# Chunked cross-attention on one core: SP issues a period's transfers in another order, two of them paced by the query projections

## What is computed

```python
def proj(t, W, b):
    t = t.transpose(0, 2, 1) @ W.T + b
    return t.reshape(N, nc, CHUNK, H, Dh)
qh = proj(q, Wq, bq); kh = proj(k, Wk, bk); vh = proj(v, Wv, bv)      # q = k = v = ctx
scores = jnp.einsum('bnqhd,bnkhd->bnhqk', qh, kh) * scale
scores = scores + jnp.where(km[:, :, None, None, :] > 0, 0.0, NEG)    # km: the mask by chunk
attn = jax.nn.softmax(scores, axis=-1)
out = jnp.einsum('bnhqk,bnkhd->bnqhd', attn, vh).reshape(N, T, C)
out = (out @ W_out.T + b_out).transpose(0, 2, 1) * masks
out = out + x
mu = jnp.mean(out, axis=2, keepdims=True)
var = jnp.mean(jnp.square(out - mu), axis=2, keepdims=True)
return (out - mu) * jax.lax.rsqrt(var + EPS)
```

## Time and profile before

| | us |
|---|---|
| median of 3 runs | 2022.49 |
| lowest and highest of them | 2009.72, 2039.61 |
| the profiled execution | 2028.28 |
| its span, first to last instruction | 2026.4 |

### The profile page before, as it was taken

The page is one execution under the profiler, slowest core; times in us unless marked ns, Lnnn a source line. Parts: engine busy times, 40 slices in busy tenths (PEclk is TensorE's granted clock), DMA queues, the critical chain, the costliest instruction groups (busy, mean ns, idle before and its releaser), DMA issues.

```text
span 2026.4 us, 90376 instructions
## 1 busy us (share of the span) xinstructions
PE 1919.8 (95%) x40488; PEld 1624.1 (80%) x40488; DVE 1703.8 (84%) x1577; ACT 1331.6 (66%) x1792; POOL 1503.6 (74%) x1059
## 2 busy tenths in 40 slices
PE   7999999999999999999999999999999999989994
PEld 6887888878788887888788888787877888878783
DVE  4887988888888887889888888887888889878796
ACT  5766766667666666766666676676666767766672
POOL 4777778777777877777777777777777778767774
PEclk9999999999999999999999999999999999999997
DMA  5667878778777887777878778787877878868666
GB/s 167 170 169 195 216 209 217 200 203 215 207 193 212 216 222 186 197 203 210 212 198 216 208 211 211 198 221 202 208 189 195 213 200 214 225 189 213 193 170 194
DMA packets 242880, 409.59 MB, mean 202 GB/s; under 512 B 28992, under 2 KB 94784, under 8 KB 242496
## 3 DMA queue, kind: packets, MB, share of 16 engines
q1 hardware_dynamic: 242496, 403.82, 75.6%
HBM read 168.82 MB, written 67.11 MB: 116 GB/s over the span
## 4 chain that ended last, share of the span: by engine, by line
PE 91%; issue 4%; DVE 2%; DMA 1%; SPq 1%; ACT 0%; POOL 0%; DVEq 0%
PE proj_bank L308 36%; PE proj_bank L365 18%; PE proj_bank L342 18%; PE score_bank L381 10%; PE o_bank L414 9%; DMA prob_t<-squares 1%; SPq L256 1%; DVE squares L668 0%; DMA b_cols<-b_in 0%; ACT prob L473 0%; DVE stats L695 0%; ACT score_bank L465 0%; DVE sums L652 0%; DVE y L686 0%; POOL prob L552 0%
## 5 line engine op out<-in xcount | busy, mean ns | idle before, releaser
L552 POOL TENSOR_TENSOR prob<-prob,recip 128x1024 f32<-128x1024 f32 x256 | 481.9, 1903 | 46.9 <-DVE recip L660 46.9
L570 POOL TENSOR_TENSOR y<-y,x_raw 128x512 f32<-128x512 f32 x256 | 330.7, 1292 | 238.4 <-DVE y L686 238.4
L560 POOL TENSOR_TENSOR ctx_lo<-ctx_raw,ctx_hi 128x512 fp32r<-128x512 f32 x255 | 330.3, 1295 | 200.3 <-ACT ctx_hi L453 187.9
L495 ACT ACTIVATE k_f<-proj_bank,b_cols 128x512 f32<-128x512 f32 x256 | 176.5, 689 | 388.3 <-PE proj_bank L308 388.3
L641 DVE TENSOR_REDUCE row_max<-score_bank 128x32 f32<-128x2048 f32 x128 | 293.3, 2292 | 162.9 <-PE score_bank L381 162.9
L308 PE MATMUL proj_bank<-ctx_hi,w_hi 128*128 128x512 f32 x1024 | 338.7, 412 | 2.9 <-DVE ctx_lo L625 2.9
L308 PE MATMUL proj_bank<-ctx_hi,w_lo 128*128 128x512 f32 x1024 | 323.3, 397 | 2.2 <-issue 2.2
L308 PE MATMUL proj_bank<-ctx_lo,w_hi 128*128 128x512 f32 x1024 | 322.2, 395 | 0.0
L652 DVE TENSOR_REDUCE sums<-prob 128x16 f32<-128x1024 f32 x256 | 309.3, 1209 | 4.2 <-ACT prob L473 4.2
L668 DVE STREAM_TRANSPOSE squares<-prob 128x2048 f32<-128x2048 f32 x128 | 294.6, 2301 | 5.2 <-POOL prob L552 2.6
L645 DVE TENSOR_TENSOR prob<-score_bank,row_max 128x2048 f32<-128x2048 f32 x128 | 293.3, 2292 | 4.4
(11 more groups left out here) (45 smaller groups left out, 3538.4 us busy)
## 6 DMA issues: line engine op xcount, KB each, us to landing
prob_t<-squares SPq DMA_DIRECT2D x1024, 128.0 KB
ctx_raw<-ctx SPq DMA_DIRECT2D x128, 512.0 KB, 7.3
x_raw<-x SPq DMA_DIRECT2D x128, 512.0 KB, 8.3
out<-y SPq DMA_DIRECT2D x128, 512.0 KB, 4.6
mask_all<-mask SPq DMA_DIRECT2D x128, 256.0 KB, 6.1
v_x<-v_f SPq DMA_DIRECT2D x256, 128.0 KB, 6.9
y<-w_in_t SPq DMA_DIRECT2D x1, 768.0 KB, 5.5
y<-w_out_t SPq DMA_DIRECT2D x1, 256.0 KB, 6.7
```

The source lines that it names most:

```text
L552: pool.tensor_tensor(part, part, half(slots(recip[:, n % 2, :]), i), ALU.mult).then_inc(norm_done, 1)
L560: pool.tensor_tensor(ctx_lo[:, n % 2, :, tokens], ctx_raw[:, n % BLOCKS, :, tokens], ctx_hi[:, n % 2, :, tokens].bitcast(F32), ALU.subtrac ...
L570: pool.tensor_tensor(part, part, x_raw[:, m % 2, f, :], ALU.add).then_inc(added, 1)
```

## The change

Only SP's `step` changes. The values are moved first, the context second; then SP waits for the first half of the query projection of block p+2 and issues the mask, waits for the second half and issues `x`; the probabilities and the store follow as before. No byte more or less is moved, and no other engine's work is touched.

```diff
             def step(p):
+
+                move_values(p + 1)
+                if p >= -2:
+                    load_ctx(p + 6)
+                if there(p + 2):
+                    sp.wait_ge(q_proj, 2 * (p + 2) + 1)
                 if p >= -1:
                     load_mask(p + 3)
-                if p >= -2:
-                    load_ctx(p + 6)
+                if there(p + 2):
+                    sp.wait_ge(q_proj, 2 * (p + 2) + 2)
                 if p >= 3:
                     load_x(p - 1)
-                move_values(p + 1)
                 move_probs(p)
```

## The result

The changed kernel takes 1941.94 us (median; 1936.52 to 1947.65) against 2024.42 of the kernel before, measured beside it: a ratio of 0.962, 95% interval 0.958 to 0.967. It is 3.8% faster. Some executions of one and the same kernel come out a few per cent longer, at a lower granted clock; every ratio in this document leaves them out, so it can differ from the ratio of the medians.

What follows compares the result with a forecast made beforehand. The prediction took PE to bound the kernel, with 93 us lost to waits for late packets of code and mostly to the clock otherwise. Its terms: 2028.3 - 38 - 18 + 5 = 1977 us, range 1945 to 2028.

Steps and rivals of the forecast that it cites:

- step 1: SP's two added waits, mask at S + 6.0 and `x` at S + 7.4 (S: start of the scores): cost nothing.
- Steps 2 and 3: Mask and `x` loaded later but landing in time, values and context moved earlier: cost nothing, gain nothing.
- Step 4: Code packet at L414 (probabilities times values) with fewer transfers ahead: 2.0 us off each wait, 38 us gained (bounds 11, 47).
- Step 5: Granted clock: with four fifths of the waits gone, most of its loss goes too, 18 us gained (bounds 4, 25).
- Step 6: Code packet for the scores, L381: later `x` adds 0.4 us to each of 14 waits, 5 us lost.
- A: Rival: the code packet is late for its own reason, SP's burst doesn't matter; nothing changes, 2015 to 2040 us; chance 0.20.
- B: Rival: values and context still hold up the code packet, 0.5 to 1 us off each wait, 1990 to 2012 us; chance 0.20.
- C: Rival: 3.1 us off, scores' waits shorter too as the chain of late packets breaks, 1955 down to 1945 us; chance 0.14.
- D: Rival: slower, since `x` at S + 7.4 stands ahead of the scores' code packet, 2057 us; chance 0.08.

Runs made afterwards that it cites:

- before_lead: The kernel before with 64 more instructions in the trace (met waits, 128 intended) at the head of PE's stream: 2073.22 us, ratio 1.045.
- before_lean_x: The kernel before with each `x` load from the third on cut to 16 of 512 columns, order and waits kept: 1931.39 us, ratio 0.973.
- all_late: The changed kernel with values, context, mask and `x` all waiting for the second half of the query projection: 2172.03 us, ratio 1.095 to the kernel before.
- order_only: The changed kernel without its two added waits (values, context, mask, `x` back to back): 1940.31 us, ratio 0.968 to the kernel before.
- x_last: The kernel before with one swap, the values ahead of `x`, no added waits: 2029.84 us, ratio 1.004.

## Why the prediction was right, and where its numbers were off

**What bounds the kernel.** Right: PE, with 93 us lost to late packets of code and to the clock behind them; the clean period did not change. before_lead shows directly that the waits are packets of code.

**The packet waits for what SP has issued.** Right: before_lean_x took away bytes and the stalls went; all_late moved the burst onto other packets and they became late. The arithmetic of step 1 (mask at S + 6.0, `x` at S + 7.4, SP's waits free) came out to a tenth of a us; only the margin is 2.8 us, from the end of L308 to that of L414 (1.40 + 1.41 in a clean period), and not "at least 3". Steps 2 and 3: PE has no wait for mask, `x` or context in the middle, as forecast.

**Step 4, the gain at L414.** 38 us forecast, 42.0 measured (48.2 to 6.2). The size was right, the reason half wrong, so that the size is in part luck: I credited it to `x` and mask going out late, behind the request. order_only holds neither back and has 1.8 us left. The count of bytes ahead of one request explains neither that nor x_last, where fewer bytes were ahead and nothing was gained. What the step missed is that the order also changes how long the same bytes take, 94.9 ns a packet against 101.1, and that one late packet makes the next late: in the stalled period of before the packet ahead of it started at S + 2.3, in the clean one at S - 0.1, and the counts above show the same over the whole run, 22 stalls behind 26 late packets and 1 behind the other 33.

**Step 5, the clock.** 18 us forecast, 18.8 by the record of the granted clock; the busy time fell by 26.4, and the rest is not accounted for. Behind the stall that ended at 1014.50 the clock was at its lower level from 1015.74 to 1019.15; the 13 such stretches became 2, as nearly all long stalls are gone.

**Step 6, the packet for the scores.** This is the step that came out the wrong way. I put down a loss of 5 us, since `x` goes out at least 2.9 us later; measured is a gain of 15.3 us, all of it. I treated the drain of the burst as fixed at 256 GB/s, so that a later `x` could only end later. `x` now lands 4.8 us after S + 7.4, S + 12.2; before, issued ahead of S + 4.5 and landing 8.3 us later, it was there by S + 12.8. The burst does not end later, and what is left of it at S + 9.3 is `x` and the end of the mask, with no values behind them. This packet is also the first of the chain above, which the step did not see: what it gains is passed on to L414. Twenty of the 36 us between the forecast (1977) and the profiled run (1940.8) are this term; 4 are step 4, 8 the busy time (step 5 and the unexplained rest), and the last 4 are small waits and the head and tail.

**The rivals.** A fell with before_lean_x and all_late. The Trainium skill, "DMA: Bandwidth & Descriptors", section "Queues, rings and completion order", has a DMA engine change to another queue after each packet, and calls a packet typically 9 to 17 descriptors, at most 64. If what the profile counts as a packet is such a descriptor, which no run here shows, that is by estimate 0.9 to 1.8 us at the 94.9 to 104.1 ns of the table, and 6 to 7 us at the most. In all_late such a packet started 4.3 us after PE had entered the block ahead, where the least in before is 0.8: the 3.5 us between them are more than the typical estimate and less than the greatest. So these runs show that code waits for several us behind data, and do not show that the rule fails. B (half the gain) did not come. C, shorter waits among the scores and the breaking of the chain of late packets, is what happened: it gave 1955, down to 1945, and had 14%; the median is 3 us below even that. D did not come here, and all_late shows that it is real: `x` alone at S + 7.4 is harmless, all four transfers there cost 9%.

The Trainium skill, "Runtime: NRT & Kernel Launch", section "Instruction fetch mechanics", calls the crossing of a block of code "mostly hidden". That holds for the changed kernel, with 6.2 us of such waits left at L419, and not for its predecessor with 63.5, or for before_lead with 114.5: it depends on what else the DMA engines have to do at that time.

## What to carry to other kernels

When PE waits on issue at the same instructions every period, look for the packet of instructions that starts just before it goes on, and ask what was issued to the DMA engines before it was due: the length of that queue is then part of PE's critical path, although no semaphore says so. Try the order of the transfers first; here it gave, within the error, all that order and pacing gave together, and pacing taken too far cost 9%. And measure a padding at the head of the stream as well: 64 instructions more, a quarter of a packet, made the kernel 4.5% slower. Look at more than the packet that stalls: here the one that started the trouble was mostly two packets earlier.

## What the runs showed of the hardware that I had not expected

The same 242,496 packets and 403.82 MB took 94.9 to 104.1 ns each, depending only on the order and the timing in which SP issued the transfers (and in one case on the mask's source). Issued 3 us later, `x` landed no later. And transfers that were only held back, with no byte added, made a kernel 9% slower, much of it by PE waiting for its own code: 143.4 us of such waits (62.9 + 43.0 + 37.5) in place of 65.7. Last, a kernel can be made 4.5% slower by 64 instructions at its head that wait for nothing.
